# A decoder layer on one core: the second half's first batch takes its row maxima from natural scores, TensorE's loop begins in the middle of the heads, and the second head's scores stand further apart

## The chip, the cores and the metric

The kernel runs on one core of a Trainium2 chip. The metric is the device time of one execution in microseconds (us): 1925.07 us, median of 3 runs (1924.38 to 1926.57). TensorE (PE) multiplies, VectorE (DVE) and ScalarE (ACT) do the elementwise work, GpSimd (POOL) and SyncE (SP) help; SP issues the DMAs. The engines run beside each other and meet at semaphores.

## The reference, cut to what matters

```python
x = layernorm(x + self_attention(x))          # 16 heads over 8 positions, relative position terms
x = layernorm(x + cross_attention(ctx, x))    # 8 heads of 64, 512 x 512 scores, masks
x = layernorm(x + ffn(x))                     # 512 -> 2048 -> 512, values rounded to 8-bit floats
# cross attention, for each of 8 batches b of 512 rows:
k, v = split((ctx @ W_src.T + b_src) * mask)              # computed in the first half of the kernel
q    = (x @ W_tgt.T + b_tgt) * mask
s    = where(mask[keys] == 0, -inf, q_h @ k_h.T / 8)      # h = 0..7
out  = concat(x, softmax(s) @ v_h) @ W_out.T + b_out
# feed-forward: relu(x @ w1.T + b1) -> 8-bit, @ w2.T (8-bit) + b2
```

Inputs and outputs are 32-bit floats: x is (8, 512, 512), ctx (8, 512, 1024).

## The kernel before, in words

The kernel has two halves. The first, up to about 820 us of the span, does the self-attention and the keys and values of the cross-attention, and is not touched. The second, `phase_b`, does the rest for 8 batches of 512 rows. A 32-bit product is made of three 16-bit ones, high and low parts apart: hi·hi, lo·hi and hi·lo.

**One head of cross-attention.** PSUM has eight banks of 128 x 512: four for scores (`st_b`), two for the feed-forward (`ff_b`), one for values (`av_b`), one for maxima (`mr_b`). Scores are made turned, keys on the partitions: `first_scores` (L1230) multiplies high parts of queries with both parts of keys, one 128 x 512 matmul for each of four key tiles. The softmax needs the maximum of each query's row, and here that runs across partitions. So DVE folds the four banks into one tile `top` (`tops`, L1593 and three L1598), TensorE turns it in four pieces (`turned_tops`, L1237), DVE takes the minimum of the negated rows (`negated_maxima`, L1603), TensorE turns the four columns into one row (`maximum_row`, L1244), and ACT copies that row into row 64 of `q2` (L1424). `second_scores` (L1251) then adds `k2`·`q2` into the same four banks: the low part of the queries, and the negated maximum against a row of ones. ACT takes exponentials (L1452), rounds them to 16 bits (`p_hi`, L1420), DVE makes the low part (`p_lo`, L1549), and `values` (L1263, L1264, L1266: 48 small matmuls) multiplies with the values. The scores of head h+1 are made while head h is in its exponentials.

**What fills TensorE beside the heads.** In batches 1 to 7 it is the feed-forward of the batch before: `feed_forward1(b, f, i, j)` issues matmuls i to j of the twelve of hidden tile f, L1203 into `ff_b`, two tiles for each head. In batch 0 there is no batch before, and the transposes of the feed-forward weights stand there (`weight_transposes`, L1196, four 128 x 128 matmuls for w1 and four for w2, two such tiles for each head; ACT scales them, L1420 and L1436, and DVE makes the low part, L1553). Their inputs come by DMA into four buffers.

**What sets the order.** Each engine has its order written out by hand. TensorE's program is: weights' transposes, `queries_and_first_scores(0)`, `heads(0)`, and then a loop of seven turns (`pe.Fori(0, 7)`, L1404) over `output_rest(b)`, `queries_and_first_scores(b + 1)`, `heads(b + 1, b)`, and the last batch's rest. `heads` ends with `output_x1` (48 matmuls of 512 columns), and the loop's branch comes behind it. `output_rest` waits for the output tiles, the queries wait for `x1T`, which SP turns by DMA transposes (L1076) once `output_x1` has used the old one.

In the loop, the second head of a batch (h = 1) is prepared in this order: two feed-forward matmuls, `first_scores` 0, two, `first_scores` 1, `first_scores` 2, two, `first_scores` 3, six, `turned_tops`. For later heads the 48 matmuls of `values` stand between scores 1 and 2. Each `first_scores` waits until the exponential of the head before has read that bank.

## Time and profile before

| | us |
|---|---|
| median of 3 runs | 1925.07 (1924.38 to 1926.57) |
| the profiled execution | 1928.58, span of its trace 1926.8 |
| TensorE busy in the span | 1799.6 (93%) |
| VectorE busy | 1377.1 (71%) |
| ScalarE busy | 768.2 (40%) |
| GpSimd busy | 559.3 (29%) |

In the views below a time is counted from the start of the span, and "L1251" is line 1251 of the kernel before. The list in order of time puts neighbours of one kind together: "x4" is four instructions, the second number the time from the start of the first to the end of the last. Brackets give the idle time of the engine just ahead, and who ended it. A 512-column matmul is shown with 0.38 us, but the next one starts 0.22 us behind it, since they are pipelined. "issue" is idle time in which the engine waited for nothing that the profile shows.

### The profile page before, as it was taken

The numbers are of one execution on the slowest core, as the hardware profiler recorded it, in microseconds if no ns is written. First come the engines' busy times: TensorE is split into PE (matmuls) and PEld (weight loads), VectorE is DVE, ScalarE is ACT, GpSimd is POOL, SyncE is SP. The second block draws the span as 40 slices with busy tenths as digits, with TensorE's granted clock in tenths as the row PEclk, the third lists the DMA queues.
The fourth block names the chain that finished last, engine by engine and source line by source line (L and its number), as shares of the span: only waits on it lengthen the run. The fifth ranks groups of instructions, "written<-read, shape, count | busy, mean of one in ns | idle before, by whom it ended". The sixth has DMA issues, their size and how long they took to land. (4 is left out here: it accounts for less than half of the span.)

```text
span 1926.8 us, 32971 instructions
## 1 busy us (share of the span) xinstructions
PE 1799.6 (93%) x12476; PEld 994.1 (52%) x12476; DVE 1377.1 (71%) x1421; ACT 768.2 (40%) x1208; POOL 559.3 (29%) x576
## 2 busy tenths in 40 slices
PE   7999999999999989866689999999999999999988
PEld 3565465546554646444445545455454554555543
DVE  2899998999899999556547567566665775757621
ACT  3323222222222222234527456274472653736522
POOL 3135965695468335400100201102003020020010
PEclk9999999999999999977899999999999999999999
DMA  8436356525643566564151620715307135061000
GB/s 207 127 78 151 80 142 151 118 74 147 155 93 98 129 170 142 148 152 150 29 104 28 115 68 7 137 39 86 96 1 134 48 63 119 2 127 33 12 34 22
DMA packets 322654, 183.97 MB, mean 95 GB/s; under 512 B 225584, under 2 KB 278832, under 8 KB 322511
## 3 DMA queue, kind: packets, MB, share of 16 engines
q1 hardware_dynamic: 316448, 178.37, 40.3%
q10 hardware_dynamic: 6062, 3.49, 0.8%
q8 instruction: 114, 1.87, 0.4%
q14 instruction: 30, 0.24, 0.0%
HBM read 94.75 MB, written 33.55 MB: 67 GB/s over the span
## 5 line engine op out<-in xcount | busy, mean ns | idle before, releaser
L1175 POOL TENSOR_TENSOR q<-q,x_hi 128x512 f16<-128x512 f32 x28 | 41.0, 1494 | 642.8 <-ACT x_hi L1473 642.8
L1203 PE MATMUL b_ff<-x2T_hi,w1T_hi 128*128 128x512 f16 x512 | 195.3, 381 | 2.3 <-DVE x2T_lo L1549 2.3
L1203 PE MATMUL b_ff<-x2T_lo,w1T_hi 128*128 128x512 f16 x512 | 195.1, 381 | 0.0
L1203 PE MATMUL b_ff<-x2T_hi,w1T_lo 128*128 128x512 f16 x512 | 195.0, 381 | 0.0
L1598 DVE SCALAR_TENSOR_TENSOR top<-b_st,mleast,top 128x512 f16<-128x512 f32 x192 | 144.1, 751 | 59.5 <-PE b_st L1230 40.0
L1549 DVE TENSOR_TENSOR p_lo<-k,p_hi 128x1024 f16<-128x1024 f32 x128 | 162.2, 1267 | 30.8 <-ACT p_hi L1420 30.8
L1452 ACT ACTIVATE k<-b_st,mbias 128x512 f32<-128x512 f32 x256 | 161.5, 693 | 42.2 <-PE b_st L1251 42.2
L785 DVE TENSOR_TENSOR prod<-q,k 128x4096 f32<-128x4096 f32 x32 | 142.2, 4445 | 17.7 <-ACT q L661 16.9
L578 PE MATMUL sm_b<-cT_hi,wsT_hi 128*128 128x256 f16 x512 | 141.1, 276 | 13.7 <-DMA cT_lo<-rows_lo 12.4
L544 PE MATMUL pj_b<-winT_hi,xT_hi 128*128 128x512 f16 x384 | 146.8, 382 | 1.1 <-DVE winT_lo L852 1.1
L544 PE MATMUL pj_b<-winT_lo,xT_hi 128*128 128x512 f16 x384 | 146.5, 382 | 0.0
L544 PE MATMUL pj_b<-winT_hi,xT_lo 128*128 128x512 f16 x384 | 146.3, 381 | 0.0
L825 DVE TENSOR_TENSOR prod<-pr,v 128x4096 f32<-128x4096 f32 x32 | 142.4, 4450 | 1.1
L1420 ACT ACTIVATE p_hi<-k 128x1024 f16<-128x1024 f32 x128 | 128.6, 1057 | 33.1 <-PE b_av L1266 33.1
L790 DVE TENSOR_REDUCE pr<-prod 128x128 f32<-128x4096 f32 x32 | 141.1, 4410 | 0.1
L578 PE MATMUL sm_b<-cT_lo,wsT_hi 128*128 128x256 f16 x512 | 141.0, 275 | 0.0
L578 PE MATMUL sm_b<-cT_hi,wsT_lo 128*128 128x256 f16 x512 | 141.0, 275 | 0.0
L1429 ACT ACTIVATE q<-q,rstdb 128x512 f32<-128x512 f32 x64 | 52.1, 814 | 222.4 <-POOL rstdb L89 222.4
L441 POOL TENSOR_TENSOR rows_lo<-cn,rows_hi 128x512 f16<-128x512 f32 x64 | 120.0, 1881 | 61.7 <-ACT rows_hi L645 61.6
L1593 DVE TENSOR_SCALAR top<-b_st,mleast 128x512 f16<-128x512 f32 x64 | 48.0, 750 | 100.2 <-PE b_st L1230 100.2
L1203 PE MATMUL b_ff<-w2T,hq 128*128 128x512 fp8e4 x512 | 112.9, 379 | 1.0 <-ACT hq L1444 1.0
L83 POOL TENSOR_TENSOR vsb<-mvb,consts 128x1 f32<-128x1 f32 x64 | 14.8, 231 | 329.7 <-DVE mvb L1564 329.7
(269 smaller groups left out, 4385.4 us busy)
## 6 DMA issues: line engine op xcount, KB each, us to landing
cn<-in_ctx_dram SPq DMA_DIRECT2D x64, 256.0 KB, 3.1
k<-kT_scratch SPq DMA_DIRECT2D x24, 512.0 KB, 7.6
x<-in_x_dram SPq DMA_DIRECT2D x32, 256.0 KB, 3.2
x_scratch<-x SPq DMA_DIRECT2D x32, 256.0 KB, 2.1
q<-x_scratch SPq DMA_DIRECT2D x8, 1024.0 KB, 5.6
q<-x_scratch SPq DMA_DIRECT2D x32, 256.0 KB, 3.3
out_dram<-q SPq DMA_DIRECT2D x32, 256.0 KB, 4.6
xn<-in_x_dram SPq DMA_DIRECT2D x24, 256.0 KB, 2.9
```

What stands on the lines that cost most here:

```text
L441: pool.tensor_tensor(lo[:, :], row_source(kind, i), hi[:, :], ALU.subtract).then_inc(s["row_lo"], 1)
L544: pe.matmul(out, a, c, start=(j == 0 and m == 0), stop=False)
L578: pe.matmul(dst, a, z, start=(j == 0 and m == 0), stop=False)
L785: dve.tensor_tensor(prod[:, :, :], q[:, t, :].unsqueeze(1).to_broadcast([P, T, E]), k[:, :, :], ALU.mult).then_inc(s["sc_prod"], 1)
L790: dve.tensor_reduce(pr[:, t].rearrange("p h s -> p s h"), prod[:, :, :].rearrange("p s (h d) -> p s h d", h=H1), AX.X, ALU.add).then_inc(s ...
L825: dve.tensor_tensor(by_head(prod), probs, by_head(v), ALU.mult).then_inc(s["av_prod"], 1)
L1203: mm = pe.matmul(out, a, c, start=(start and n == 0), stop=end)
L1420: act.activation(dst, src, ACT.Copy, scale=scale).then_inc(done, 1)
L1429: act.activation(x2[:, tt, :], x2[:, tt, :], ACT.Identity, bias=f[:, 1:2], scale=f[:, 0:1]).then_inc(s[l + "_done"], 1)
L1452: act.activation(pf[:, st, :], st_b[st][:, :], ACT.Exp, bias=mbias[:, st:st + 1], scale=D2 ** -0.5).then_inc(s["st_exp"], 1)
L1549: dve.tensor_tensor(dst, bank, hi, ALU.subtract).then_inc(out, 1)
L1598: dve.scalar_tensor_tensor(out=top[:, :], in0=st_b[st][:, :], scalar=mleast[:, st:st + 1], in1=top[:, :], op0=ALU.add, op1=ALU.max).then_i ...
```

## The change

There are three parts.

**The first batch.** Batch 0 gets functions of its own on PE, ACT and DVE. Its maxima come from scores in natural layout, queries on the partitions (`natural_scores`, into banks 2 and 3), where a row's maximum runs along the free axis: DVE adds a mask tile `mneg` and keeps the maximum in the same instruction (`natural_tops`). `turned_tops` and the reduction go. The turned scores are then made whole, both products one behind the other (`both_scores`, into banks 0 and 1), so four 512-column matmuls more for each head. `mneg` is made once, in memory that `f16o` uses later, and `output_x1` no longer waits for the last exponential.

**The loop.** `heads` is cut in two, `first_part_of_heads` (through head 3) and `rest_of_heads` (from head 4). The loop starts with the rest of the heads and ends with the first part of the next batch's. It has six turns (`pe.Fori(1, 7)`), and one batch's worth of its body is written out ahead and behind.

**The second head.** The twelve feed-forward matmuls around `first_scores` of head 1 stand 2, 2, 4, 2, 2 and not 2, 2, 0, 2, 6.

```diff
+            def natural_scores(h, half):
+                for tt in (2 * half, 2 * half + 1):
+                    if h or tt >= 2:
+                        pe.wait_ge(s["topped"], 4 * h + tt - 1)
+                    pe.matmul(st_b[2 + tt % 2][:, :], q1[:, h, tt * P:(tt + 1) * P], k1[:, h, :], start=True,
+                              stop=True).then_inc(s["first_filled"], 1)
+            def both_scores(h, half):
+                for st in (2 * half, 2 * half + 1):
+                    if st == 0:
+                        pe.wait_ge(s["mr_copied"], h + 1)
+                    if h or st >= 2:
+                        pe.wait_ge(s["st_exp"], 4 * h + st - 1)
+                    keys = slice(st * P, (st + 1) * P)
+                    pe.matmul(st_b[st % 2][:, :], k1[:, h, keys], q1[:, h, :], start=True, stop=False)
+                    pe.matmul(st_b[st % 2][:, :], k2[:, h, keys], q2[:, h, :], start=False,
+                              stop=True).then_inc(s["st_filled"], 1)
...
-                if ff is None:
-                    pe.wait_ge(s["st_exp"], 32)
...
+                    at = 4 if h else 8
+                    if not h:
+                        feed_forward1(ff, f, 4, 8)
                     first_scores(b, h + 1, 2)
-                    feed_forward1(ff, f, 4, 6)
+                    feed_forward1(ff, f, at, at + 2)
                     first_scores(b, h + 1, 3)
-                    feed_forward1(ff, f, 6, 12)
+                    feed_forward1(ff, f, at + 2, 12)
...
+            def first_heads():
+                weight_transposes(0)
+                pe.wait_ge(s["q_masked"], 4)
+                maximum_row(0, 0)
+                for h in range(H2):
...
+                    if h + 1 < H2:
+                        natural_scores(h + 1, 0)
+                    both_scores(h, 0)
...
+                    if h:
+                        values(0, h - 1)
+                    if h + 1 < H2:
+                        natural_scores(h + 1, 1)
+                    weight_transposes(2 * h + 1)
+                    both_scores(h, 1)
+                    if h + 1 < H2:
+                        maximum_row(0, h + 1)
+                        weight_transposes(2 * h + 2)
+                output_x1(None)
+                values(0, H2 - 1)
...
-            heads(0, None)
-            with pe.Fori(0, NBATCH - 1) as b:
+            first_heads()
+            output_rest(0)
+            queries_and_first_scores(1, 0)
+            first_part_of_heads(1, 0)
+            with pe.Fori(1, NBATCH - 1) as b:
+                rest_of_heads(b, b - 1)
                 output_rest(b)
                 queries_and_first_scores(b + 1, b)
-                heads(b + 1, b)
+                first_part_of_heads(b + 1, b)
             last = NBATCH - 1
+            rest_of_heads(last, last - 1)
...
+            def natural_tops(h, half):
+                for tt in (2 * half, 2 * half + 1):
...
+                    dve.tensor_tensor_reduce(top[:, :], st_b[2 + tt % 2][:, :], mneg, 1.0, NEG, ALU.add, ALU.max,
+                                             mx[:, h % 2, tt:tt + 1]).then_inc(s["topped"], 1)
+                if half:
+                    dve.wait_ge(s["topped"], 4 * h + 4)
+                    dve.tensor_scalar(mz[:, 4 * (h % 2):4 * (h % 2) + 4, D2], mx[:, h % 2, :], -1.0, None,
+                                      ALU.mult).then_inc(s["negm"], 1)
```

On ACT the first batch's order for a head becomes two exponentials, the first rounding, one weight tile, two exponentials, the next head's maximum row, the second rounding, one weight tile. On DVE it becomes two natural maxima, the division of the head before, two natural maxima, the negation, a low part, a weight tile, a low part, a weight tile.

On DVE, in batch 0, this stood under head 1 before (with the maxima of head 2) (`top` is the folded tile, `mz` the negated maxima, `p_lo` the low part of the exponentials, `w1T_lo` that of a weight tile, `b_av` the values):

```order
L1593 TENSOR_SCALAR top<-b_st,mleast 128x512
L1598 SCALAR_TENSOR_TENSOR top<-b_st,mleast,top 128x512 x3
L1549 TENSOR_TENSOR p_lo<-k,p_hi 128x1024
L1553 SCALAR_TENSOR_TENSOR w1T_lo<-b_ff,w1T_hi 128x4x128
L1603 TENSOR_REDUCE mz<-b_mr 128x4
L1615 RECIPROCAL rden<-b_av 128x4
L1617 TENSOR_TENSOR k<-b_av,rden 128x4x64
L1549 TENSOR_TENSOR p_lo<-k,p_hi 128x1024
L1553 SCALAR_TENSOR_TENSOR w1T_lo<-b_ff,w1T_hi 128x4x128
```

and this stands there now (`mxb` holds the maxima, `f16o` is the memory of `mneg`):

```order
L1690 ISA top,mxb<-b_st,f16o 128x512
L1690 ISA mxb 128x1
L1690 ISA top,mxb<-b_st,f16o 128x512
L1690 ISA mxb 128x1
L1711 RECIPROCAL rden<-b_av 128x4
L1713 TENSOR_TENSOR k<-b_av,rden 128x4x64
L1690 ISA top,mxb<-b_st,f16o 128x512
L1690 ISA mxb 128x1
L1690 ISA top,mxb<-b_st,f16o 128x512
L1690 ISA mxb 128x1
L1694 TENSOR_SCALAR mz<-mxb 128x4
L1631 TENSOR_TENSOR p_lo<-k,p_hi 128x1024
```

The reduction L1603 is gone, and each maximum is now two instructions, the one over 512 columns and one that writes 128 x 1.

On PE, the loop's branch was here before, between the turning of the output tiles ahead of the loop and `output_rest` (`oT`):

```order
L1196 MATMUL b_mr<-ident,k 128x128 x4
L1196 MATMUL b_av<-ident,k 128x128 x4
L1404 UNCONDITIONAL_BRANCH
L1404 ISA
L1203 MATMUL b_st2<-wxT_hi,oT_hi 128x512
L1203 MATMUL b_st2<-wxT_lo,oT_hi 128x512
```

and is here now, in front of head 4's `second_scores` (`b_ff1` is a feed-forward tile of the batch before):

```order
L1206 MATMUL b_ff1<-x2T_lo,w1T_hi 128x512
L1206 MATMUL b_ff1<-x2T_hi,w1T_lo 128x512
L1468 UNCONDITIONAL_BRANCH
L1468 ISA
L1273 MATMUL b_st0<-q2,k2 128x512
L1273 MATMUL b_st1<-q2,k2 128x512
L1273 MATMUL b_st2<-q2,k2 128x512
```

What stands around a turn has moved from output products to scores and feed-forward.

On PE, in the loop, the first scores of head 1 (`b_st0` to `b_st3`, `b_ff0` a feed-forward tile) stood like this before:

```order
L1230 MATMUL b_st0<-q1,k1 128x512
L1203 MATMUL b_ff0<-x2T_hi,w1T_lo 128x512
L1203 MATMUL b_ff0<-x2T_hi,w1T_hi 128x512
L1229 REGISTER_ALU
L1230 MATMUL b_st1<-q1,k1 128x512
L1229 REGISTER_ALU
L1230 MATMUL b_st2<-q1,k1 128x512
L1203 MATMUL b_ff0<-x2T_lo,w1T_hi 128x512
L1203 MATMUL b_ff0<-x2T_hi,w1T_lo 128x512
L1230 MATMUL b_st3<-q1,k1 128x512
```

and stand like this now:

```order
L1233 MATMUL b_st0<-q1,k1 128x512
L1206 MATMUL b_ff0<-x2T_hi,w1T_lo 128x512
L1206 MATMUL b_ff0<-x2T_hi,w1T_hi 128x512
L1233 MATMUL b_st1<-q1,k1 128x512
L1206 MATMUL b_ff0<-x2T_lo,w1T_hi 128x512
L1206 MATMUL b_ff0<-x2T_hi,w1T_lo 128x512
L1206 MATMUL b_ff0<-x2T_hi,w1T_hi 128x512
L1206 MATMUL b_ff0<-x2T_lo,w1T_hi 128x512
L1233 MATMUL b_st2<-q1,k1 128x512
L1206 MATMUL b_ff0<-x2T_hi,w1T_lo 128x512
L1206 MATMUL b_ff0<-x2T_hi,w1T_hi 128x512
L1233 MATMUL b_st3<-q1,k1 128x512
```

Four of the six matmuls that came behind the last scores now come between scores 1 and 2.

## Rows read from the trace of the kernel before

**Rows 1.** The page's head and the table of stretches: five engines, clock, DMA:

```profile
span 1926.8 us, 32971 instructions
...
858.00:951.20 93.20, 57.15 (x513) 37.43 (x514) 52.71 (x75) 48.86 (x78) 0.00 (x0) 0.78 0.34 110
1000.00:1840.00 840.00, 825.37 (x6522) 428.74 (x6520) 537.65 (x812) 444.66 (x658) 95.99 (x232) 1.00 0.33 67
902.40:913.70 11.30, 6.38 (x81) 4.30 (x82) 7.69 (x12) 6.95 (x11) 0.00 (x0) 1.00 0.31 96
```

**Rows 2.** Who TensorE waited for, 1000 to 1860 us: total, times, longest:

```profile
PE b_st L1203 <- issue: 8.5, 6, 2.1
PE b_st L1230 <- ACT k L1452: 4.0, 7, 0.6
```

**Rows 3.** TensorE in order of time, first batch: start, length, idle before:

```profile
858.05 1.89 PE L1251 MATMUL b_st<-q,k 128*128 128x512 f16 x4 [0.68 <-ACT q L1424]
...
863.37 1.08 PE L1196 MATMUL b_ff<-ident,x2T_lo 128*128 128x128 f32 x4 [3.43 <-DMA x2T_lo<-in_w_dram]
...
874.73 1.89 PE L1251 MATMUL b_st<-q,k 128*128 128x512 f16 x4 [0.68 <-ACT q L1424]
...
902.39 1.04 PE L1251 MATMUL b_st<-q,k 128*128 128x512 f16 x4 [0.68 <-ACT q L1424]
...
910.25 0.40 PE L1237 MATMUL b_mr<-minus,top 128*128 128x128 f16 x4 [1.67 <-DVE top L1598]
...
913.68 1.04 PE L1251 MATMUL b_st<-q,k 128*128 128x512 f16 x4 [0.68 <-ACT q L1424]
...
951.16 1.04 PE L1251 MATMUL b_st<-q,k 128*128 128x512 f16 x4 [0.68 <-ACT q L1424]
```

**Rows 4.** VectorE by line, 903 to 951 us: busy and mean ns, idle before:

```profile
L1598 DVE SCALAR_TENSOR_TENSOR top<-b_st,mleast,top 128x512 f16<-128x512 f32 x12 | 9.0, 751 | 4.0 <-PE b_st L1230 2.9
L1603 DVE TENSOR_REDUCE mz<-b_mr 128x4 f16<-128x512 f32 x4 | 2.8, 689 | 0.0
L1615 DVE RECIPROCAL rden<-b_av 128x4 f32<-128x4 f32 x4 | 0.7, 174 | 0.0
```

**Rows 5.** TensorE in order of time, behind the first batch's heads:

```profile
954.58 0.39 PE L1203 MATMUL b_st<-wxT_hi,x1T_hi 128*128 128x512 f16 x1 [0.94 <-ACT k L1452]
...
986.63 0.58 PE L1203 MATMUL b_st<-x1T_hi,wtT_hi 128*128 128x512 f16 x1 [4.06 <-DMA x1T_lo<-q]
```

**Rows 6.** TensorE in order of time, two turns of its loop:

```profile
1224.54 0.39 PE L1203 MATMUL b_st<-wxT_hi,oT_hi 128*128 128x512 f16 x1 [2.05 <-issue]
...
1718.82 0.39 PE L1203 MATMUL b_st<-wxT_hi,oT_hi 128*128 128x512 f16 x1 [0.37 <-issue]
```

**Rows 7.** Stretches around two turns, in mid-heads, and ahead of a query:

```profile
1222.00:1225.00 3.00, 0.95 (x6) 0.23 (x4) 0.00 (x0) 0.00 (x0) 0.00 (x0) 1.00 1.23 139
1717.00:1719.00 2.00, 1.63 (x8) 0.60 (x7) 0.00 (x0) 0.00 (x0) 0.00 (x0) 1.00 0.59 72
1164.00:1174.00 10.00, 10.00 (x98) 5.35 (x97) 7.41 (x13) 6.35 (x10) 0.00 (x0) 1.00 0.01 2
1605.00:1606.00 1.00, 1.00 (x6) 0.49 (x5) 0.55 (x1) 0.58 (x1) 0.31 (x2) 1.00 0.43 164
1606.00:1607.00 1.00, 1.00 (x7) 0.43 (x5) 0.84 (x2) 0.24 (x1) 0.00 (x0) 1.00 0.00 0
```

**Rows 8.** TensorE in order of time, the queries behind the fifth turn:

```profile
1607.61 0.38 PE L1203 MATMUL b_st<-x1T_hi,wtT_hi 128*128 128x512 f16 x1
```

**Rows 9.** The second head of a batch in the loop, in order of time:

```profile
1132.54 0.75 DVE L1593 TENSOR_SCALAR top<-b_st,mleast 128x512 f16<-128x512 f32 x1 [2.53 <-PE b_st L1230]
1133.43 2.53 DVE L1598 SCALAR_TENSOR_TENSOR top<-b_st,mleast,top 128x512 f16<-128x512 f32 x3
1133.72 0.39 PE L1230 MATMUL b_st<-q,k 128*128 128x512 f16 x1 [0.57 <-ACT k L1452]
...
1136.01 0.40 PE L1237 MATMUL b_mr<-minus,top 128*128 128x128 f16 x4
```

More of the change, by code:

```diff
@@ L1323, in heads, with some_heads @@
                 feed_forward1(ff, 1, 6, 12)
-                for h in range(H2):
+                some_heads(b, ff, range(0, H2 // 2))
+            def some_heads(b, ff, which):
+                for h in which:
                     second_scores(b, h)
@@ L1351, in heads, with rest_of_heads @@
                     feed_forward1(ff, f + 1, 7, 12)
+            def rest_of_heads(b, ff):
+                some_heads(b, ff, range(H2 // 2, H2))
                 feed_forward2(ff, 0)
                 feed_forward2(ff, 1)
-                if ff is None:
-                    output_x1(ff)
                 values(b, H2 - 1)
@@ L1361, in heads @@
                     transposes(tq_b[tt], o[:, tt, :], s["ot_filled"])
-                if ff is not None:
-                    output_x1(ff)
+                output_x1(ff)
+            def first_heads():
[3 more added lines that the diff above has]
+                for h in range(H2):
+                    for g, (i, _) in enumerate(GROUPS):
+                        for a in range(2):
+                            if h + 1 == 2 * i + a:
+                                pe.wait_ge(qs_ld[g][a], 48)
+                    if h + 1 < H2:
+                        natural_scores(h + 1, 0)
+                    both_scores(h, 0)
+                    if h == 1:
+                        pe.wait_ge(s["v_ld"], 80)
+                    if h:
[9 more added lines that the diff above has]
+                values(0, H2 - 1)
+                pe.wait_ge(s["o_norm"], 8)
+                for tt in range(4):
+                    transposes(tq_b[tt], o[:, tt, :], s["ot_filled"])
             def output_rest(b):
@@ L1370, in output_rest, with first_queries_and_scores @@
                              (w.ones[:, 0:P], rows_b[:, :]), s["om_filled"], start=False)
+            def first_queries_and_scores():
+                for i in range(3):
+                    queries(0, i, first=True)
+                queries(0, 3, slice(None, 8))
+                pe.wait_ge(s["k_ld"], 48)
+                pe.wait_ge(qs_ld[0][0], 48)
+                natural_scores(0, 0)
+                queries(0, 3, slice(8, None))
+                natural_scores(0, 1)
             def queries_and_first_scores(b, ff):
                 for i in range(3):
-                    queries(b, i, first=ff is None)
-                if ff is not None:
-                    x2_transposes(ff)
+                    queries(b, i)
+                x2_transposes(ff)
                 queries(b, 3, slice(None, 8))
-                if ff is not None:
-                    pe.wait_ge(s["x2t_lo"], 4 * ff + 2)
+                pe.wait_ge(s["x2t_lo"], 4 * ff + 2)
                 pe.wait_ge(s["q_masked"], 4 * b + 2)
@@ L1445, in relu, with exponentials @@
                                saturate=False).then_inc(s["relu"], 1)
-            def exponentials(b, h, half):
+            def exponentials(b, h, half, banks=4):
                 for st in (2 * half, 2 * half + 1):
@@ L1517, in _ @@
             first_x1_high()
-            for i in range(3):
+            for i in range(4):
                 queries_hi(0, i)
@@ L1521, in _ @@
             act.wait_ge(s["rows_made"], 4)
-            heads(0, None)
+            first_heads()
             def batch(b, rows):
@@ L1659, in heads, with first_heads, first_queries_and_maximum @@
                     low(col(oT[1], tt), bank4(tq_b[tt]), col(oT[0], tt), s["ot_hi"], 4 * b + tt + 1, s["ot_lo"])
+            def first_heads():
+                w1_low(0)
+                for h in range(H2):
+                    if h + 1 < H2:
+                        natural_tops(h + 1, 0)
+                    if h:
+                        normalized(0, h - 1)
+                    if h + 1 < H2:
+                        natural_tops(h + 1, 1)
+                    exponentials_low(0, h, 0)
+                    w1_low(2 * h + 1)
+                    exponentials_low(0, h, 1)
+                    if h + 1 < H2:
+                        w1_low(2 * h + 2)
+                normalized(0, H2 - 1)
+                for tt in range(4):
+                    low(col(oT[1], tt), bank4(tq_b[tt]), col(oT[0], tt), s["ot_hi"], tt + 1, s["ot_lo"])
+            def first_queries_and_maximum():
+                queries_masked(0, 0)
+                queries_low(0, 0)
+                queries_masked(0, 1)
+                queries_low(0, 1)
+                queries_masked(0, 2)
+                natural_tops(0, 0)
+                queries_low(0, 2)
+                queries_masked(0, 3)
+                natural_tops(0, 1)
+                queries_low(0, 3)
             def queries_and_first_maximum(b, ff):
@@ L1714, in _ @@
             masks(0)
-            queries_and_first_maximum(0, None)
-            heads(0, None)
+            first_queries_and_maximum()
+            first_heads()
             with dve.Fori(0, NBATCH - 1) as b:
```

76 lines of the change are left out of this document (43 added, 33 removed).

## The prediction, as it was written before the changed kernel ran

> **What bounds the kernel now.** I read the table of stretches first, then who TensorE waited for, then single heads in order of time. From 1000 to 1840 us TensorE is busy for 825 of 840 us at a full clock [rows 1]: in the loop only TensorE's own idle time can be won, and the list of its waits names nearly all that there is, 8.5 us in six pieces of "issue" ahead of `output_rest`, and 4.0 us in seven pieces on an exponential [rows 2]. The first batch's heads are another regime. From 858 to 951.2 us TensorE is busy for 57 of 93 us with a granted clock of 0.78, VectorE for 53, ScalarE for 49 [rows 1]. Nobody is full, so a chain through all three decides. In its fast state a head takes 913.68 − 902.39 = 11.3 us from one `second_scores` to the next [rows 3], and in it VectorE works 7.69, ScalarE 6.95 and TensorE 6.38 us [rows 1]. The reader sees the chain in the gaps: TensorE waits 1.67 us for the last `top` ahead of L1237, and from that turning (910.25) to the next second scores (913.68) another 3.4 us go by, for the turning, reduction, second turning and copy of the maximum.
>
> **First batch: what goes, comes and moves.** Per head, VectorE loses the reduction (0.69) and four `tops` (4 × 0.75) [rows 4]; TensorE loses four small turnings (0.40 us, [rows 3]) and gains four 512-column matmuls at 0.22 us each, 0.9. ScalarE does the same work. Most of all, the scores of the next head no longer share banks with those of this one, so the maxima can be taken while the exponentials run.
>
> The price of one natural maximum is in no row. It is two instructions, and I bound it by the nearest rows: below by one `tops` alone, 0.75; above by twice that for the main part and the reduction's 0.69 for the second, 2.2 us. I take 0.75 + 0.17 = 0.92, the second part like the smallest instruction, the reciprocal [rows 4], since the first reads the same PSUM bank at the same width as L1598. VectorE's work for a head is then 7.69 − 0.69 − 3.00 + 4 × 0.92 + 0.17 (the negation) = 7.85 us. Behind each maximum comes a wait on VectorE's own semaphore: three L1598 take 2.53 us in a row, 0.14 more apiece than their 0.75 [rows 9]; five such waits are 0.7. The second low part also waits some 0.2 us for ScalarE's second rounding, which now stands behind the maximum row. Sum 8.8 us. ScalarE's 6.95 and TensorE's 6.38 + 0.9 − 0.4 = 6.9 fit under it, so VectorE becomes the bound, and 11.3 becomes 8.8.
>
> [...]
>
> At half clock TensorE would bind instead. [...] Before, the clock fell while TensorE stood idle nearly half of a fast head (busy 6.38 of 11.3). After it is busy 6.9 of 8.8 when fast and always when slow, so I expect it fast for most heads. I take 15% of the six head periods at 12: 0.85 × 8.8 + 0.15 × 12 = 9.3 us.
>
> The two ends of the stretch. The first second scores come at 858.05 [rows 3]. The new path to them drops the turning and the reduction and has the negation (0.17) in their place, and the query tile that the copy was queued behind on ScalarE comes earlier: about 3.3 us, bounds 1 (only the two steps that go) and 5; 854.8. The step from head 0 to head 1 took 16.7 us and held waits for weight DMAs (3.43 us at 863.37, [rows 3]). SP issues these loads behind the query copies, which wait for the last low query part; that comes earlier by some 2 us of the 3.3, an estimate. With the DMA still last, the weights are turned near 864.3 and head 1's scores start at 865.1 (bounds 863 and 869, where the loads gain nothing). Head 7 then starts at 865.1 + 6 × 9.3 = 920.9, not at 951.16: 30.3 us earlier.
>
> Behind it, 951.16 to 986.63 was 35.5 us, ending in the DMA-turned `x1T` of batch 1 [rows 5]. This tail hangs on head 7's values, which follow `output_x1`. That started 3.4 us after the second scores; now the second pair of whole scores stands ahead of it, behind a weight tile, for about 4.3 us. That costs 0.9. The wait on the last exponential that is taken off `output_x1` buys nothing, as the scores ahead of it need ScalarE anyway. The mask tile (one 128 x 512 operation ahead of the first queries) lies in time in which VectorE waits for them: nothing, or 0.4 if that cover goes. First batch: 30.3 − 0.9 = 29.4 us.
>
> **The loop's turn.** The six pieces of "issue" are not alike. At 1224.54 the idle time is 2.05 us, at 1718.82 only 0.37 [rows 6]; the six add up to 8.5. Around the long one the DMA engines are at 1.23 busy share, around the short one at 0.59 [rows 7]: SP is pushing DMA transposes of `x1` there. In mid-heads, where the turn goes, the share is 0.01 and TensorE is busy for 10.00 of 10 us [rows 7]. So a turn should cost there what the cheap one did, 0.37, or with some traffic 0.45 (bounds 0.3 and 2.05), five times: 2.2 us.
>
> [...]
>
> What is late next is `x1T`. The queries behind the fifth turn start at 1607.61 [rows 8]; the DMA engines are still at 0.43 in the microsecond from 1605 and at 0.00 from 1606 [rows 7], so the transposes landed about 1.6 us ahead of need. They are paced by `output_x1` and SP's stores, not by the turn. With the about 1.9 us of such a turn gone ahead of the queries, TensorE comes a few tenths too early: I charge 0.3 for each of seven batches (bounds 0 and 1), 2.1. The loop's gain is 8.5 − 2.2 − 2.1 = 4.2 us.
>
> **The second head.** TensorE waits 0.57 us for the exponential ahead of scores 2 at 1133.72, 4.0 us over seven batches. Four matmuls in front of it (0.86 us) will cover that. But look where it led: `turned_tops` starts at 1136.01, and VectorE's last `top` ends at 1133.43 + 2.53 = 1135.96 [rows 9]. That chain began at 1132.54 with the first scores and ran without a gap, so TensorE already ended on it. From the first scores to `turned_tops` TensorE has 14 matmuls, 3.0 us, against some 3.9 of that chain. Now all twelve feed-forward matmuls are gone earlier and TensorE waits about 0.9 us at `turned_tops`. Gain 0; bounds −1 and +1 us in all.
>
> **The sum** against the profiled execution: 1928.58 − 29.4 − 4.2 − 0 = 1895.0. That execution lay 3.5 us above the median of 1925.07, so in the median's terms **1891.5 us**.
>
> **Rivals.**
> [...]
> - Slow maximum: the part over 512 columns takes twice 0.75, 3.0 us more per head: 11.8. For it: it must keep an accumulator, which L1598 does not. Against: the same sources and width. With 2 us more ahead of head 1, head 7 comes at 937.9: 1908.5. [...]
> - The turn's cost doesn't go: it costs as much in mid-heads, or comes back whole as a wait for `x1T`. For it: the 1.6 us of slack. Against: the cheap turn at 1718.82. 1925.07 − 29.4 = 1895.7.
> - Slower: the maximum's serial price. VectorE pays it four times in each head, and from 8.8 + 4 × 1.5 = 14.8 us a head on, head 7 starts no earlier than before and the loop's 4.2 is used up; that is 2.4 us for one maximum, beyond my upper bound of 2.2. At 3 us a head takes 17.1 and the time is about 1925 − 4 + 0.9 + (865.1 + 102.6 − 951.16) = 1938. For it: only that no row shows it.
>
> **How the numbers follow.** Forecast 62%, with an own range of 1884 to 1900; clock 9%; slow maximum 10%; turn's cost stays 15%; slower 3%; the rest lies outside, to both sides. At the low end a head takes 8.3 us in every period (35.4 + 4.2 + 2 more from the turns), about 1884; I go to 1881, for the first path's bound. The high end takes in the clock and the slow maximum: 1908. A median of this kernel can be told from no change from about 0.2%, 3.9 us. All cases but the last are faster by more: faster 0.94, same 0.03, slower 0.03.
>
> **What would show it.** Right: the first scores of heads 1 to 7 about 9 us apart, VectorE nearly without idle time there, and the stretch before the loop 30 us shorter; "issue" ahead of L1273 in mid-heads at some 0.4 us five times; small waits for DMA at the queries; the wait on the exponential replaced by one on `top` at L1259 of about 0.9 us, with batches no shorter for it. Wrong: natural maxima far from 0.9 us; a granted clock under 0.8 in the first batch; mid-head turns near 2 us; batches shorter by more than what the turn gave.

## The result, and the profile after

The changed kernel takes 1902.2 us (median of 4, 1901.9 to 1905.5), the kernel before 1925.8 on the same chip: a ratio of 0.9877, 95% interval 0.9856 to 0.9898. The forecast was 1891.5 us. The time lies in the whole range of 1881 to 1908 us, but outside the forecast's own of 1884 to 1900; the gain is 23.6 us and not 33.6, and two terms of the sum were far off in opposite directions. In the profiled executions the spans are 1926.8 and 1900.2 us, 26.6 apart. Cut at four points of TensorE's program:

| Stretch of TensorE's program | before, us | after, us | change | forecast |
|---|---|---|---|---|
| start to head 7's second scores of the first batch | 951.16 | 917.37 | -33.8 | -30.3 |
| from there to the first query of the second batch (waits for `x1T`) | 35.47 | 34.75 | -0.7 | +0.9 |
| from there to the second batch's first second scores | 21.57 | 19.18 | -2.4 | 0 |
| the rest of the span, the loop in it | 918.6 | 928.9 | +10.3 | -4.2 |

The first batch gave 36.9 us, 7.5 more than forecast; the loop part took 10.3 back.

The page's head and the table of stretches (TensorE, its weight loads, VectorE, ScalarE, GpSimd, then granted clock, DMA share, GB/s), the counterparts of [rows 1]; the second row is one period of the first batch's heads:

```profile
span 1900.2 us, 32993 instructions
...
858.00:951.20 93.20, 75.36 (x724) 46.03 (x722) 58.40 (x122) 60.23 (x94) 8.30 (x16) 0.95 0.56 148
893.30:901.50 8.20, 6.78 (x82) 4.53 (x81) 6.88 (x16) 7.22 (x12) 0.00 (x0) 1.00 0.43 128
1000.00:1820.00 820.00, 802.14 (x6273) 416.49 (x6270) 512.76 (x777) 422.15 (x624) 96.40 (x232) 0.99 0.30 66
```

A head has 8.2 us now, with 11.3 before, at a granted clock of 0.95 in the stretch instead of 0.78. The fullest engine in this period is ScalarE (7.22 us), not VectorE (6.88). In the long stretch TensorE now stands idle for 17.9 of 820 us, before for 14.6 of 840.

Who TensorE waited for in 1000 to 1830 us, the counterpart of [rows 2] (total, times, longest):

```profile
PE b_st L1273 <- issue: 11.7, 5, 2.5
PE b_mr L1259 <- DVE top L1681: 4.8, 6, 0.8
```

The first is the loop's turn, which now stands ahead of `second_scores` of the fifth head: 2.3 us each, five times, not 0.45. The second is the second head's wait, moved from the exponential to `turned_tops` as forecast (0.8 us; a seventh lies outside the stretch).

VectorE by line in 890 to 915 us, the counterpart of [rows 4]:

```profile
L1690 DVE CUSTOM_DVE_ANT_0 top<-b_st,f16o 128x512 f16<-128x512 f32 x13 | 8.9, 686 | 1.0
L1631 DVE TENSOR_TENSOR p_lo<-k,p_hi 128x1024 f16<-128x1024 f32 x7 | 8.5, 1221 | 2.9 <-ACT p_hi L1486 2.9
```

L1690 is the natural maximum's main part, 0.686 us; its second part takes 0.08, and from one maximum to the next go 0.83 us. Such a VectorE is not full: it waits 0.96 us a head for ScalarE's `p_hi`. TensorE, in order of time, the counterparts of [rows 3, 5]:

```profile
862.36 0.47 PE L1199 MATMUL b_ff<-ident,x2T_lo 128*128 128x128 f32 x1 [3.40 <-DMA x2T_lo<-in_w_dram]
...
866.89 0.63 PE L1251 MATMUL b_st<-q,k 128*128 128x512 f16 x1
...
893.29 0.38 PE L1251 MATMUL b_st<-q,k 128*128 128x512 f16 x1
...
901.47 0.38 PE L1251 MATMUL b_st<-q,k 128*128 128x512 f16 x1
...
917.37 0.38 PE L1251 MATMUL b_st<-q,k 128*128 128x512 f16 x1
...
952.12 0.38 PE L1206 MATMUL b_st<-x1T_hi,wtT_hi 128*128 128x512 f16 x1 [1.92 <-DMA x1T_lo<-q]
```

The weight DMA ahead of head 1 is as late as before (3.40 us). The heads' second scores start at 855.12, 866.89, 876.75, 885.19, 893.29, 901.47, 909.63 and 917.37.

One turn of the loop, in order of time, then the stretches during the stall, behind it, and behind a dear turn of the kernel before; these answer to [rows 6, 7]:

```profile
1253.42 0.41 PE L1266 MATMUL b_mr<-ident,mz 128*65 128x128 f16 x4
...
1254.52 0.38 PE L1206 MATMUL b_ff<-x2T_hi,w1T_lo 128*128 128x512 f16 x1
1257.14 1.72 PE L1273 MATMUL b_st<-q,k 128*128 128x512 f16 x4 [2.24 <-issue]
1258.66 0.63 PE L1206 MATMUL b_ff<-x2T_hi,w1T_hi 128*128 128x512 f16 x1
...
1260.78 0.38 PE L1233 MATMUL b_st<-q,k 128*128 128x512 f16 x1
```

```profile
1254.90:1257.10 2.20, 0.00 (x1) 0.00 (x0) 0.13 (x1) 0.00 (x0) 0.00 (x0) 1.00 0.00 0
1257.10:1260.80 3.70, 3.66 (x10) 1.34 (x11) 0.62 (x1) 3.00 (x5) 0.00 (x0) 0.54 0.02 4
```

```profile
1224.50:1228.00 3.50, 3.46 (x17) 1.58 (x17) 0.35 (x1) 0.00 (x0) 0.00 (x0) 1.00 1.00 309
```

The stall is only a little over half of the price. Behind it the granted clock is 0.54 for 3.7 us: 3.7 x 0.46 = 1.7 us more. Behind the old turn of 2.05 us it stayed at 1.00. From one `output_rest` to the next a batch takes 123.57 us before and 126.14 after (means over four). DMA, whose absence I had counted on, is absent indeed, at 0.00 in the stall.

In every turn of both kernels one packet of the instruction queue, q8, starts between the start of the branch and the first matmul behind it. I read it as the fetch of the code behind the branch. This is the DMA view of two stretches of 0.2 us, first of the kernel before, 1221.60 to 1221.80, then of the one after, 1254.50 to 1254.70 (queue, kind: packets, MB, share of 16 engines):

```profile
q1 hardware_dynamic: 226, 0.05, 151.7%
q8 instruction: 1, 0.02, 36.2%
```

```profile
q8 instruction: 1, 0.02, 30.6%
```

A packet of this queue is some 16 KB (1.75 MB in 107 on the page). Narrow stretches like these give the start of each turn's packet. From its start to the first matmul behind the turn go 2.5 to 2.9 us, in both kernels, busy queues or none: 1221.7 to 1224.54 before, 1254.6 to 1257.14 after. The trace also records the branch on TensorE's sequencer (`PEldq`, `COMPARE_BRANCH`; the duration stands three times, in ns, then the start). These are a dear turn and the cheap one of the kernel before, then a turn of the one after:

```profile
L1404 PEldq COMPARE_BRANCH  x1: 5817/5817/5817, 1218.6 to 1218.6; - x1
L1404 PEldq COMPARE_BRANCH  x1: 4133/4133/4133, 1714.5 to 1714.5; - x1
L1468 PEldq COMPARE_BRANCH  x1: 3408/3408/3408, 1253.6 to 1253.6; - x1
```

Set against the modelled end of the last matmul ahead of it, the branch begins 3.93 us ahead in all six turns of the kernel before, and only 1.3 us ahead in all five of the one after. That is the difference between the two places. The difference between dear and cheap turns of the kernel before is another one: from the start of the branch to the start of its packet go 1.8, 3.2, 3.1, 2.9, 3.1 and 1.6 us, and in the kernel after 0.9 to 1.0.

### The profile page after: what moved, and what is told of

It is laid out like the page before. It is cut to its first block and busy times, and to the rows that moved or that the text cites. A ratio compares the mean times of both kernels' runs of the same rounds, so it can differ in the third digit from the quotient of the medians.

```text
span 1900.2 us, 32993 instructions
## 1 busy us (share of the span) xinstructions
PE 1796.0 (95%) x12476; PEld 991.4 (52%) x12476; DVE 1370.5 (72%) x1454; ACT 771.0 (41%) x1208; POOL 556.8 (29%) x576
## 3 DMA queue, kind: packets, MB, share of 16 engines
q8 instruction: 107, 1.75, 0.4%
## 5 line engine op out<-in xcount | busy, mean ns | idle before, releaser
L1681 DVE SCALAR_TENSOR_TENSOR top<-b_st,mleast,top 128x512 f16<-128x512 f32 x168 | 126.1, 751 | 54.6 <-PE b_st L1233 39.3
L441 POOL TENSOR_TENSOR rows_lo<-cn,rows_hi 128x512 f16<-128x512 f32 x64 | 120.0, 1881 | 63.1 <-ACT rows_hi L645 63.0
L1676 DVE TENSOR_SCALAR top<-b_st,mleast 128x512 f16<-128x512 f32 x56 | 42.0, 750 | 99.6 <-PE b_st L1233 99.6
```

The lines of the kernel that those rows point to most:

```text
L441: pool.tensor_tensor(lo[:, :], row_source(kind, i), hi[:, :], ALU.subtract).then_inc(s["row_lo"], 1)
L1681: dve.scalar_tensor_tensor(out=top[:, :], in0=st_b[st][:, :], scalar=mleast[:, st:st + 1], in1=top[:, :], op0=ALU.add, op1=ALU.max).then_i ...
```

## The experiments

All runs are compared with the kernel before on their own chip; "a batch" is the mean of four from `output_rest` to `output_rest`, and "lead" is from the packet's start to the modelled end of the last matmul ahead of the branch: how far ahead of it the branch began, less the time until its packet started.

**1. The first part alone** (`e1`), and **2. the old turn with both other parts** (`e2`):

```diff
-            output_rest(0); queries_and_first_scores(1, 0); first_part_of_heads(1, 0)
-            with pe.Fori(1, NBATCH - 1) as b:
-                rest_of_heads(b, b - 1)
+            with pe.Fori(0, NBATCH - 1) as b:
                 output_rest(b)
                 queries_and_first_scores(b + 1, b)
                 first_part_of_heads(b + 1, b)
+                rest_of_heads(b + 1, b)
```

(here and in the fences below cut to what matters; for the first, also `at = 4` for every head and no feed-forward tile 4 to 8 ahead of head 1's scores)

> The first batch alone is changed (row maxima from natural scores); the loop turns where it did before, and the second head keeps its old spacing. From the two traces the first batch and the tail behind it give 36.9 us, and the loop part gives back 10.3 us (918.6 us before, 928.9 after). If the first batch is independent of the rest, this runs in 1925 - 37 = 1888 us. If what the loop part loses comes from the first batch (the clock or the buffers with which it enters the loop), it stays at 1900. The last span of the loop part should be 918 to 919 us by the first theory, 928 by the second.

> The changed kernel with the loop's turn back ahead of the second half's first head; the other two parts stay. Theory A (the turn in mid-heads costs 2.3 us of stall and a spell at half clock, five times): 1888 to 1890 us, turns again 0.4 to 2.0 us with no fall of the clock behind them. Theory B (the loss comes from the wait that the second head now has for turned_tops, 0.80 us seven times = 5.6 us): the loss stays, 1894 to 1898 us, and the first kernel of this set is 5 to 10 us faster than this one.

Measured: 1886.4 us (ratio 0.9786, 0.9764 to 0.9809) and 1885.5 (0.9783, 0.9761 to 0.9806). The new place of the turn costs 1900.2 - 1883.7 = 16.5 us of span against the old one in the same kernel; five times 126.14 - 122.76 = 3.4 is 16.9. The second head's spacing is worth nothing: a batch takes 122.79 without and 122.76 us with it, as theory A and the prediction had it. The surprise is in the old turns. They cost 0.2 to 1.1 us, not 1.8 to 2.05, in a loop whose code had not changed:

```profile
PE b_mr L1259 <- DVE top L1677: 4.8, 6, 0.8
PE b_st L1206 <- issue: 3.2, 6, 0.9
```

So the forecast's kernel before was not the right yardstick: of the 42 us that the second run gains, 8.5 - 3.2 = 5.3 are cheaper turns. Theory A's time of 1888 to 1890 us was missed by that.

**3. The turn behind `feed_forward2`'s second piece**, with 32 matmuls and no wait ahead of the branch (the four later heads and both pieces move from `rest_of_heads` to `first_part_of_heads`):

```diff
-                some_heads(b, ff, range(0, H2 // 2))
+                some_heads(b, ff, range(0, H2))
+                feed_forward2(ff, 0)
+                feed_forward2(ff, 1)
```

> The turn stands behind the last projection of feed-forward (feed_forward2, second piece) of the batch, so that 32 matmuls of 512 columns with no wait between them stand ahead of the branch. Lead theory (the fetch behind the branch takes about 2.9 us in every place, and TensorE loses only what its sequencer was not ahead of the array by): the stall is below 0.5 us, the clock keeps its level, and the time is 1888 - 5 x 1.3 = about 1881 to 1885 us. Rival (a turn costs about 2.3 us wherever it stands away from its old place): five stalls of 2.3 us and the half clock behind them, 1900 us. Rival (the fetch is slowed by the core's DMA traffic): the stall follows the DMA share at that point, and is 1.8 us if that is as high as at the old place, 0.4 if not, so 1881 to 1890.

Measured: 1908.7 us (0.9901, 0.9878 to 0.9924), worse than all my theories. TensorE in order of time; the branch lies at 1291.13, where nothing stops, and the stall comes after 28 of the values' 48 matmuls:

```profile
1291.96 0.19 PE L1285 MATMUL b_av<-v_hi,p_hi 128*128 128x65 f16 x1
1294.85 0.24 PE L1286 MATMUL b_av<-v_lo,p_hi 128*128 128x64 f16 x1 [2.70 <-issue]
```

The lead theory is right about the branch: its packet starts at 1288.1, 3.0 us ahead, and the branch costs nothing. But a second packet starts at 1292.3, 2.6 us ahead of 1294.85. As I read it, the target lay 28 matmuls with their weight loads, 56 instructions, ahead of the end of its 16 KB block, and the next block was not asked for in time. That stall is 2.1 to 4.1 us.

**4. No loop**: run 2's kernel with `for b in range(NBATCH - 1):` in place of `with pe.Fori(0, NBATCH - 1) as b:`.

> TensorE's loop is written out, seven batches in a row, so that it has no branch at all. If the turns' stalls are the whole of the difference between the places of the turn, this takes the old turns' 8.5 us (less than that where a later wait takes their place) off the kernel with the old turn: 1880 to 1884 us, with no idle time put down to issue above 0.3 us. Rival (code that runs once is fetched as dearly as code behind a branch): many small issue gaps all along the part, and a time of 1890 us or more.

Measured: 1883.7 us (0.977, 0.9742 to 0.9798); no issue gap in the loop part; a batch takes 121.98 us, the floor against which all other turns can be priced: before 1.6 a batch, changed kernel 4.2, old turn in run 2 0.8. Its page has 99 instruction packets (run 2's 114), and in the loop part no stall at any of them. Its executions spread from 1877.3 to 1890.0 us. The profiled span gains only 1.5 us on run 2; its first batch has a DMA wait of 5.08 us for the weights, which run 11 takes up.

**5. The turn in mid-heads ahead of `maximum_row`**:

```diff
                     feed_forward1(ff, f + 1, 0, 7)
+                    if h + 1 == H2 // 2:
+                        return
                     maximum_row(b, h + 1)
...
             def rest_of_heads(b, ff):
 
+                maximum_row(b, H2 // 2)
+                feed_forward1(ff, H2 + 1, 7, 12)
                 some_heads(b, ff, range(H2 // 2, H2))
```

> The changed kernel with the loop's turn moved up a little in mid-heads: it stands ahead of maximum_row for the fifth head, so that seven matmuls of 512 columns (1.5 us), not five behind the row's wait, lie between the last wait of TensorE and the branch. Theory A (the code behind the branch always takes 2.6 to 3.1 us to come; the array stands still for that less what the sequencer was ahead of it, and a wait shortly before the branch takes the lead away): the block of code is asked for 1 to 1.5 us ahead of the array's last matmul instead of 0.4, and the stall falls from 2.3 to 1.2 to 1.8 us; 1893 to 1899 us, the lower end if the clock no longer falls behind it. Theory B (a turn in mid-heads costs 2.3 us wherever it is): 1902 us as the changed kernel.

Measured: 1918.6 us (0.9942, 0.9925 to 0.996). TensorE's turn:

```profile
1257.12 0.38 PE L1206 MATMUL b_ff<-x2T_hi,w1T_hi 128*128 128x512 f16 x1
1259.53 0.41 PE L1266 MATMUL b_mr<-ident,mz 128*65 128x128 f16 x4 [2.04 <-issue]
1262.48 0.58 PE L1206 MATMUL b_ff<-x2T_lo,w1T_hi 128*128 128x512 f16 x1 [2.54 <-issue]
```

The branch begins 1.75 us ahead instead of 1.3, the lead grew from 0.3 to 0.4 us to 0.7 to 0.8 (in one turn 0.3), not to 1 to 1.5, and the stall fell from 2.33 to 2.09 on the mean: the right direction, under its size. And a second stall is here too, 2.4 to 3.1 us, after four matmuls: by the same reading this target lay 8 instructions ahead of a block's end. The kernel as changed has it some 18 instructions later, at the beginning of a block. It was spared that by luck.

**6. The kernel before, its transposing DMAs held until the turn is past**:

```diff
                     for tt in half:
                         store(b, tt)
+                    if half == (0, 1):
+                        sp.wait_ge(s["om_filled"], 4 * b + 5)
+                        stand_alone(sp, alone["sp"])
```

> The kernel before, with one thing changed: SyncE's four transposing DMAs of x1 (two rows of tiles) wait until TensorE has filled the first tile behind the turn, so that they are not under way while TensorE's code is fetched. Theory C (in the kernel before the fetch of the last block ahead of the branch is held up by these DMAs, which start 6.8 to 7.2 us ahead of the turn, and so TensorE's sequencer comes to the branch late): the turns' stalls of 1.8 to 2.05 us fall to 0.2 to 0.6 us, and the time by about 4 x 1.4 = 5 to 6 us to 1920 us, unless the later transposes make TensorE wait for x1T. Theory D (the place of the code in its blocks alone decides): the stalls stay at 1.8 to 2.05 us and the time at 1925 to 1927 us.

Measured: 1969.2 us (1.0219, 1.0192 to 1.0245), slower by the price I had only mentioned:

```profile
PE b_st L1206 <- DMA x1T_lo<-q: 40.0, 6, 6.8
```

The question is answered all the same. TensorE's instructions are those of the kernel before, and no turn has any issue gap:

```profile
1225.62 0.38 PE L1206 MATMUL b_ff<-wxT_hi,x1T_lo 128*128 128x512 f16 x1
1225.93 0.39 PE L1206 MATMUL b_st<-wxT_hi,oT_hi 128*128 128x512 f16 x1
```

The lead is 2.9 to 3.0 us in all six turns, and it just covers the 2.8 to 2.95 us from the packet's start to the first matmul behind the turn. With the transposes under way it was 2.1, 0.8, 0.9, 1.0, 0.8 and 2.4. Yet the branch begins where it did, 3.93 us ahead of the last matmul's end:

```profile
L1407 PEldq COMPARE_BRANCH  x1: 3699/3699/3699, 1222.1 to 1222.1; - x1
```

What the held transposes took away is the time until its packet starts, 0.95 to 1.06 us now. Theory C's DMAs are to blame, but not by making the sequencer late.

**7. The same DMAs ahead of the stores, on run 2's kernel** (the two `for tt in half` loops of `store` and `turn_x1` change places):

> The counterpart: the kernel with the turn at its old place (1885.5 us, turns of 0.2 to 0.9 us), but SyncE issues the four transposing DMAs ahead of the two stores instead of behind them, so that they start 8 us ahead of the turn rather than 5.8 us, at the time at which the last block of code ahead of the branch is asked for. Theory C (collision of that fetch with the transposes): stalls of 1.5 to 2 us, and 1885.5 + 5 x 1.4 = 1892 us. Theory D (place of the code alone): stalls and time as they are, 1885 us.

Measured: 1910.4 us (0.9904, 0.9878 to 0.9929), but not for the turns, which cost 0 to 0.5 us. The stores came late and with them the residual and `x2T_lo`:

```profile
PE b_st L1233 <- DVE x2T_lo L1627: 17.1, 6, 3.0
```

Neither theory's number. The run misses its own condition: the transposes started 7.7 us ahead of the turn, and the last ordinary block had been asked for 7.9 to 8.6 us ahead of it, just before them.

**8. The kernel before, its code shifted by 16 instructions**:

```diff
+            for _ in range(16):
+                stand_alone(pe, alone["pe"])
             for n, (src, _, _) in enumerate(jobs):
```

> The kernel before, with 16 more instructions on TensorE (increments of a semaphore nobody waits for) ahead of the second half's first matmul: nothing in the loop changes but where its code lies in the 16 KB blocks; the 16 cost at most 1 to 2 us themselves, once. Theory D (the place of the code in its blocks decides how late the last block ahead of the branch is asked for): the turns fall from 1.8 to 2.05 to 0.3 to 1 us, the time to 1920 to 1922 us. Theory C (transposes alone): the stalls stay at 1.8 to 2.05 us, the time at 1926 us.

Measured: the turns cost 0.46, 0.88, 0.47, 0.40, 1.26 and 0.39 us, 3.9 in all instead of 8.5, and a batch takes 122.86 us instead of 123.57. That is theory D's number for the stalls. The time is 1925.7 us (0.9987, 0.9974 to 1.0001), as the 16 instructions cost 2.4 us at the start of the half, and the interval takes in no change at all. The profiled span fell from 1926.8 to 1921.5.

Runs 6 to 8 together: in runs 1, 2 and 6 to 8 the branch begins 3.8 to 3.9 us ahead of the last matmul's end in every turn, as in the kernel before, so no dear turn has a sequencer that came late. Only the time from the branch to its packet differs: 0.95 to 1.06 us in run 6, 1.1 to 1.5 in run 7, 0.9 to 2.4 in runs 1, 2 and 8, and 2.9 to 3.2 in the four dear turns. Two things stand together in these four. The transposes are under way, and the last ordinary block's packet starts within 1.5 us ahead of the branch. Such a late block without the transposes costs nothing (five turns of run 6), and transposes with a block 3.6 to 4.8 us ahead leave turns of 0 to 1.3 us (runs 1, 2, 7 and 8). The two turns left of the kernel before lie between, with blocks at 1.8 and 3.3 us and turns of 0.56 and 0.37. Why the packet starts late when both meet, I didn't see.

**9. One natural maximum more for each head of the first batch**, on run 2's kernel:

```diff
+                    if h and tt == 3:
+                        dve.tensor_tensor_reduce(top[:, :], st_b[3][:, :], mneg, 1.0, NEG, ALU.add, ALU.max,
+                                                 mx[:, h % 2, 3:4]).then_inc(s["step"], 1)
+                        dve.wait_ge(s["step"], 5 + h)
```

> The kernel with the turn at its old place (1885.5 us) with VectorE taking one natural maximum more for each of seven heads of the first batch (the last tile's, 0.69 + 0.08 us and its pitch, 0.84 us; the same values twice). Theory V (as predicted, VectorE's own work bounds the first batch): 7 x 0.84 = 5.9 us longer, the period of a head 9.0 us instead of 8.2, time 1891 us. Theory X (the ring of ScalarE's row and exponentials, VectorE's low parts, TensorE's values bounds it, and VectorE has a spare wait of 0.96 us a head for ScalarE's p_hi): 0 to 2 us longer, time 1885 to 1888 us, and the wait for p_hi shrinks by what the maximum takes.

Measured: 1890.8 us (0.9816, 0.979 to 0.9841), 5.2 more than run 2, near theory V's number. But the steady periods became 9.6 to 9.8 us from 8.16, more than V's 9.0, and the granted clock in them is 0.85 to 0.86 and not 1.00, so part of each is the clock's:

```profile
892.33:902.07 9.74, 7.82 (x81) 5.03 (x80) 7.40 (x18) 7.11 (x11) 0.00 (x0) 0.85 0.33 109
```

And the wait for `p_hi` only halved, which V doesn't explain. Hence the counterpart:

**12. One maximum less** (for each head but the first, the last tile's maximum becomes a copy of the third's, `tensor_scalar(mx[:, h % 2, 3:4], mx[:, h % 2, 2:3], 1.0, ...)`):

> The counterpart of the run with one maximum more: the kernel with the turn at its old place (1885.5 us), in which VectorE doesn't take the last tile's natural maximum for seven heads of the first batch and copies the third tile's instead (one small operation of 0.16 us, so 0.66 us less a head; this part of the computation is left out). One maximum more cost 5.3 us (1890.8). Theory V (VectorE's maxima lie in the ring that sets a head's time, and no other ring is close): 7 x 0.66 = 4.6 us less, 1881 us. Theory G (another ring, through ScalarE's row, exponentials and TensorE's values, is as long as it is now, so that more work shows and less doesn't): 1884.5 to 1886 us.

Measured: 1887.2 us (0.9784, 0.9768 to 0.98; run 2 0.9783). The steady period is 8.16 us in both: taking 0.66 us off VectorE buys nothing. Theory G: VectorE's chain is at par with another ring. The other ring can be read gapless in the changed kernel's trace, where one period is from the first row to the last:

```profile
893.21 1.23 DVE L1631 TENSOR_TENSOR p_lo<-k,p_hi 128x1024 f16<-128x1024 f32 x1 [0.96 <-ACT p_hi L1486]
894.50 0.20 PE L1285 MATMUL b_av<-v_hi,p_hi 128*128 128x65 f16 x1 [0.18 <-DVE p_lo L1631]
896.17 1.06 ACT L1486 ACTIVATE p_hi<-k 128x1024 f16<-128x1024 f32 x1 [0.72 <-PE b_av L1288]
897.41 0.60 ACT L1486 ACTIVATE w1T_hi<-b_ff 128x512 f16<-128x512 f32 x1 [0.18 <-PE b_ff L1199]
897.90 0.59 ACT L1505 ACTIVATE w2T<-b_ff 128x512 fp8e4<-128x512 f32 x1
898.38 1.27 ACT L1519 ACTIVATE k<-b_st,mbias 128x512 f32<-128x512 f32 x2
899.68 0.59 ACT L1493 ACTIVATE q<-b_mr 1x512 f16<-1x512 f32 x1
900.29 1.06 ACT L1486 ACTIVATE p_hi<-k 128x1024 f16<-128x1024 f32 x1
...
901.38 1.23 DVE L1631 TENSOR_TENSOR p_lo<-k,p_hi 128x1024 f16<-128x1024 f32 x1 [0.96 <-ACT p_hi L1486]
```

Low part, values (to 896.13), `p_hi`, two weight tiles, two exponentials, row copy, `p_hi`: 8.17 us with VectorE in it only once.

**10. Run 3's kernel, its code shifted by 72 instructions** (the increments stand at the end of the first half):

```diff
+            for _ in range(72):
+                stand_alone(pe, s["made"])
```

> The kernel with the turn behind the second piece of feed_forward2 (1908.7 us; no stall at the branch itself, but 2.1 to 4.1 us after the first 28 matmuls behind it) with 72 instructions more on TensorE at the end of the first half (increments nobody waits for; at 0.15 us each up to 10.8 us, part of it hidden by the wait between the halves). They move the branch's target from 56 instructions ahead of the end of a 16 KB block of code to the beginning of the next. Theory E (behind a branch only the target's block comes; the next is asked for only when that one is there, so the array stands still if little of the target's block is left): no stall of over 0.5 us in the loop, no half clock behind it; the part from the second batch on is as long as in the kernel with the old turn, and the time 1884 us plus up to 8 us that the 72 cost once. Theory F (the stalls belong to the place between feed_forward2 and the values, not to the code's position): five stalls of 2 to 4 us stay, 1909 us or more.

Measured: 1884.3 us (0.9779, 0.9756 to 0.9803) against 1908.7, 24 us from instructions that do nothing. One issue gap of 0.22 us is left, a batch takes 122.43 us instead of 127.26. The stalls are gone, as theory E said, and with them theory F.

**11. The best version: no loop, and the first batch's residual rows loaded behind weight tile 8**:

```diff
-            for tt in range(4):
-                load_residual(0, tt, True)
             for n in range(4, FT):
                 load_weights(n)
+                if n == 8:
+                    for tt in range(4):
+                        load_residual(0, tt, True)
```

> The candidate for the best version: the kernel with TensorE's seven batches written out (1883.7 us), and in SyncE's queue the four loads of the residual rows of the first batch stand behind the feed-forward weights' tile 8 instead of ahead of tile 4. In the unrolled kernel's trace the weights' tiles of heads 1 to 3 come 1.3, 0.3 and 5.1 us late (in the changed kernel 3.4, 1.7 and 1.5). If the residual rows' 1 MB is what delays them: 2 to 5 us less, 1879 to 1882 us. If it is the loads of the queries, or the x1 rows just ahead: no change, 1884 us.

Measured: 1877.4 us (0.9739, 0.9719 to 0.976), 6.2 less than run 4 (5.6 by the spans, 1876.6 and 1882.2) and a little under my range. Of the weights' waits one is left:

```profile
860.58 0.66 PE L1200 MATMUL b_ff<-ident,x2T_lo 128*128 128x128 f32 x4 [2.48 <-DMA x2T_lo<-in_w_dram]
```

## Why the prediction was right and wrong, step by step

**The first batch: right in most of its mechanism, mis-sized.** "VectorE becomes the bound, and 11.3 becomes 8.8", with 15% of half clock 9.3: measured 8.16 in the steady state and 8.41 as mean of the six periods. One maximum, put at 0.92 and up to 0.14 of waiting, costs 0.83 all told. That is 4 x 0.23 = 0.9 us a head less on VectorE, and alone it would have given 7.9. The period is 8.16, and VectorE idles 0.96 us of it, where "nearly without idle time" was the sign of being right: by runs 9 and 12 VectorE is only one of two bounds, and the ring through ScalarE is as long. The clock term (15% at half clock, 0.5 us a head) was mostly not needed; the stretch's clock is 0.95. The 12 us of a head in it stand in no run. The longest period behind head 1 in the changed kernel is 9.86 us, at a granted clock of 0.85 and with a DMA wait of 1.5 us in it, and the last four are 7.74 to 8.18 us at 1.00. The maximum isn't slow either: its main part, in the trace as `CUSTOM_DVE_ANT_0`, takes 0.686 us against L1598's 0.75 [rows 4].

**The ends of the stretch: right.** Head 0 at 855.12 (forecast 854.8), head 1 at 866.89 (865.1), with the DMA still last.

**The tail: small and wrong in sign.** +0.9 was forecast, -0.7 came, and a term was missing: the wait for `x1T` is 1.92 us instead of 4.06 [rows 5], and the queries behind it ran 2.4 us faster, at a granted clock of 1.00 where it was 0.89 before.

**The loop's turn: the step that failed.** It read "so a turn should cost there what the cheap one did, 0.37, or with some traffic 0.45". It cost 2.33 us, and 1.7 more in lost clock, of which I had nothing. I had looked at what lay beside a turn (DMA share) and not at what lay ahead of it on TensorE. In the old place 48 products whose waits were met long before stand ahead of the branch, and it begins 3.93 us ahead of the last one's end. In mid-heads the sequencer waits for the maximum, has the row's four small matmuls and five large ones left behind that, and the branch begins 1.3 us ahead. From there to the first matmul behind the turn go 3.5 to 3.8 us with the DMA queues idle, which leaves the stall of 2.15 to 2.50. Run 6 shows that DMA traffic does matter at the old place, so the comparison of 1.23 with 0.59 [rows 7] was not empty; it just isn't what is paid in the new place. The rival "its cost doesn't go" came closest, at 1.8 to 2.05; it had no clock in it. In every turn of both kernels a packet of its own starts behind the branch, 2.5 to 2.9 us ahead of the first matmul behind the turn. Five times the dearest turn of the kernel before, 2.05 us, would be 10.25 us; measured are 11.7, plus 8.5 for the clock.

**The wait for `x1T` in the loop: wrong.** 2.1 us were charged; none appeared. That isn't only because TensorE's turns had not become cheaper: in run 4, without any turn, no wait for `x1T` stands in the loop part either.

**The second head: right.** 0.80 us at `turned_tops` (forecast 0.9) in place of 0.57 at the exponential, gain 0.

**Sum.** -36.9 for -29.4, +10.3 for -4.2: the errors of 7.5 and 14.5 us have opposite signs, and half of the second was hidden by the first. With the first batch as forecast the time would have been about 1902.2 + 7.5 = 1909.7 us, outside the range: that it lies inside is luck.

What stays open: why 16 instructions made the old turns cheap. The branch's packet starts late where a late block and the transposes meet; run 6 isolates the transposes, and no run moves the block alone (run 8 shifts all the code behind its 16 instructions).

## What to carry to other kernels

A loop's turn on TensorE cost, in these runs, the time from the branch's start to the first matmul behind it (3.5 to 4.1 us with quiet DMA queues, up to 6.0 beside DMA transposes), less how far ahead of the last matmul's end the branch began (3.9 us at most, 1.3 shortly behind a wait). So put it behind a long run of matmuls without a wait, keep the kernel's own DMA bursts away from it where that is free (in run 6 it cost 42 us), and look at the granted clock behind the stall before pricing it (0.54 for 3.7 us behind 2.24 us here). Then look for a second stall a few matmuls behind the turn (28 in run 3, 4 in run 5), which I read as a target near the end of its block: in run 10 filler instructions ahead of the loop took it away and were worth 24 us. Where code size allows, write the loop out. And price a change against a kernel whose other turns may move by luck: the same turns cost 8.5 us in the kernel before and 3.9 with its code shifted by 16 instructions.

## What the hardware showed that I had not expected

- Behind a branch the next block's packet starts only 0.3 to 2.4 us after the first matmul behind the turn (all kernels with a loop). In runs 3 and 5, where by my reading 56 and 8 instructions of the target's block were left, a second stall of 2.1 to 4.1 us followed; with the target of run 3 moved by 72 instructions (run 10) it did not.
- The branch never began more than 3.93 us ahead of the modelled end of the last matmul, and its packet never more than 3.0.
- After the changed kernel's five stalls of 2.15 to 2.50 us the granted clock was 0.52 to 0.59 in the next 3.5 us; after the four of 1.81 to 2.05 us before it stayed at 1.00. In run 3 it stayed at 1.00 behind 2.14 us and was 0.50 to 0.60 behind the four of 2.69 to 4.13.
- Sixteen increments of a semaphore lengthened TensorE's idle time at the start of the half from 4.76 to 7.20 us, 0.15 each.
